# Output projection, norm, route and scatter of a mixture-of-experts layer joined into one stage, and its experts in pieces

## What is computed

```python
h = layernorm(x) * (1 + ca) + sa
x = x + ga * ((mamba(x_f) + flip(mamba(flip(x_b)))) @ w_out.T + b_out)      # two directions
h = layernorm(x) * (1 + cb) + sb
scores = softmax(h @ wg)                       # 8 experts
top1 = argmax(scores); rank = running count of tokens of the same expert
slot = top1 * 641 + rank                       # capacity 641, later tokens are dropped
y = gelu(buf[slot] @ W1[e] + b1[e]) @ W2[e] + b2[e]       # 128 -> 512 -> 128
x = x + gb * where(rank < 641, y[slot], 0) * scores[top1]
```

## Time and profile before

| | us |
|---|---|
| median of 3 runs | 1871.85 (1871.12 to 1874.78) |
| profiled execution | 1881.69, its span 1879.9 |
| busy: TensorE, VectorE, ScalarE, GpSimd | 1542, 1341, 1012, 1009 |
| mamba stage | 0 to 924 |
| projection and norm | 924 to 962 |
| route and scatter | 962 to 1021 |
| experts | 1021 to 1151 |
| attention, norm, experts of layer 1 | 1151 to 1880 |

### The profile page before, as it was taken

The page is one execution under the profiler, slowest core; times in us unless marked ns, Lnnn a source line. Parts: engine busy times, 40 slices in busy tenths (PEclk is TensorE's granted clock), DMA queues, the critical chain, the costliest instruction groups (busy, mean ns, idle before and its releaser), DMA issues. The chain is left out here.

```text
span 1879.9 us, 22117 instructions
## 1 busy us (share of the span) xinstructions
PE 1542.2 (82%) x7115; PEld 706.3 (38%) x7115; DVE 1341.4 (71%) x1497; ACT 1011.8 (54%) x1645; POOL 1008.5 (54%) x534
## 2 busy tenths in 40 slices
PE   7777887878878787886691886898899998899998
PEld 4222222222222222221271664554455555464443
DVE  6599999999999999999562112666666776157545
ACT  4867777777667777764230432444555555456221
POOL 1599999999999999999524333211011110025000
PEclk8899889898998989887875997879999999889999
DMA  4464443243444443333014222522333320102546
GB/s 155 102 158 103 113 102 92 81 108 81 112 113 102 113 102 94 84 98 90 26 35 113 48 67 61 143 54 63 86 87 87 85 72 20 51 1 50 120 100 139
DMA packets 101777, 164.94 MB, mean 88 GB/s; under 512 B 16678, under 2 KB 55374, under 8 KB 99990
## 3 DMA queue, kind: packets, MB, share of 16 engines
q1 hardware_dynamic: 93510, 159.07, 33.5%
q0 software_dynamic: 2688, 4.80, 0.8%
q10 hardware_dynamic: 5504, 0.09, 0.2%
HBM read 106.32 MB, written 26.04 MB: 70 GB/s over the span
## 5 line engine op out<-in xcount | busy, mean ns | idle before, releaser
L484 POOL TENSOR_TENSOR PR<-H,CS 128x1024 f32<-128x1024 f32 x256 | 598.4, 2359 | 50.9 <-DVE H L460 19.0
L460 DVE TENSOR_TENSOR_SCAN H<-DA,X 128x1024 f32<-128x1024 f32 x192 | 431.1, 2273 | 0.0
L349 PE MATMUL psY<-PR,fold 128*64 128x512 f32 x1024 | 295.4, 671 | 7.0 <-POOL PR L484 7.0
L448 DVE TENSOR_TENSOR X<-DU,psB 128x1024 f32<-128x1024 f32 x192 | 235.7, 1228 | 51.1 <-PE psB L328 25.6
L436 ACT ACTIVATE DA<-DT,negA 128x511 f32<-128x511 f32 x384 | 250.7, 710 | 1.1
L1478 ACT ACTIVATE a_PT<-a_psS 128x512 f32<-128x512 f32 x320 | 181.1, 601 | 110.3 <-PE a_psS L1382 106.2
L1525 DVE TENSOR_REDUCE a_MX<-a_psM 128x1 f32<-128x384 f32 (+3 forms) x352 | 203.6, 635 | 25.1 <-PE a_psM L1397 23.8
L1396 PE MATMUL a_psM<-a_kst,a_qst 72*128 72x512 bf16 (+3 forms) x512 | 140.2, 321 | 14.3 <-DVE a_MX L1525 10.5
L495 POOL TENSOR_TENSOR XS<-DU,BS 128x1024 f32<-128x1024 f32 x64 | 150.8, 2356 | 0.0
L298 PE MATMUL pp<-work,convW 128*128 (+1 forms) x256 | 140.8, 680 | 8.9 <-ACT pre L389 8.6
L460 DVE TENSOR_TENSOR_SCAN H<-X,XS 128x1024 f32<-128x1024 f32 x64 | 146.1, 2283 | 1.6 <-POOL XS L495 1.3
(11 more groups left out here) (293 smaller groups left out, 2624.8 us busy)
## 6 DMA issues: line engine op xcount, KB each, us to landing
CS<-c_rows SPq DMA_DIRECT2D x128, 256.0 KB, 3.9
DT<-W SPq DMA_DIRECT2D x64, 256.0 KB, 4.4
DU<-ab SPq DMA_DIRECT2D x64, 256.0 KB, 4.3
BS<-c_rows SPq DMA_DIRECT2D x64, 256.0 KB, 4.2
g_CB<-c_tok SPq DMA_DIRECT2D x32, 512.0 KB, 11.1
scratch_q<-a_partsq SPq DMA_DIRECT2D x24, 384.0 KB, 3.3
a_qst<-scratch_q SPq DMA_DIRECT2D x8, 1152.0 KB
a_kst<-scratch_k SPq DMA_DIRECT2D x24, 384.0 KB
```

Source lines behind the costliest of these rows:

```text
L349: last = nc.tensor.matmul(psY[h * HP:(h + 1) * HP, n % 2 * T:(n % 2 + 1) * T], fold[:, :], chunk(PR[n % 4], h), start=False, stop=n >= NS - 2)
L448: nc.vector.tensor_tensor(both(X[s % 2][:, :]), DU[p][:, at:at + 2, :], psB[:, :].unsqueeze(1).to_broadcast([P, 2, T]), ALU.mult).then_inc ...
L460: nc.vector.tensor_tensor_scan(H[s % 4][:, :], decay, x, 0.0, ALU.mult, ALU.add).then_inc(scan_done, 1)
L484: nc.gpsimd.tensor_tensor(both(PR[s % 4][:, :]), both(H[s % 4][:, :]), CS[q % 2][:, s // 2 % 2, :].unsqueeze(1).to_broadcast([P, 2, T]), A ...
```

## The change

- **One stage by batches.** `MambaOutputs` and `route_stage` go, and `outputs_stage` does projection, norm, choice, placing and scatter in one pipeline of 11 steps. Step n projects batch n, computes the variance and rows of batch n - 1, logits and transposes of batch n - 2; in odd steps from 3 on VectorE chooses for a group, in even ones from 4 on it places one, in pieces between the batch's own operations. b_out * gate is made once (`gb`) and added to xT by ScalarE ahead of time (`act_bias`); the residual is one VectorE operation from PSUM. GpSimd only scatters. wo, xc, rb, var, psPN and tps have one bank each, psL two. SP loads pack2 at the start, pack3 when the last projection is done.
- **Experts.** The slots are cut by pairs of experts (11, 10, 10, 10 tiles). Only the first piece is transposed ahead; the groups of pair i + 1 stand between the hidden tiles of pair i. One bank for transposes instead of two, three for results instead of two. The loops are written out. The first two experts' weights are issued by ScalarE at the start; SP issues the ids behind the slots.
- **Mamba's prologue.** Loads, ScalarE's and VectorE's steps stand in another order, Silu's table is loaded by a small activation of its own, and c_rows is always stored between DT's and DU's loads.

```diff
 # program
-            with ExitStack() as outputs:
-                layernorm_stage(nc, "ln1", W, xT, hT, modv(0, 4), modv(0, 3), (W2, ins["pack2"]),
-                                MambaOutputs(nc, outputs, W, XP, xT, modv(0, 2)))
-            route_stage(nc, W, W2, hT, slots, cw, W3, ins["pack3"])
+            outputs_stage(nc, W, W2, ins["pack2"], XP, xT, hT, mod[:, 0, 2, :], modv(0, 2), modv(0, 4), modv(0, 3), slots, cw, W3, ins["pack3"])
 # outputs_stage
+        def pe_project(pe, b):
+            if b >= 1:
+                pe.wait_ge(x_ready, b)
...
+        def pe_center(pe, b):
+            pe.wait_ge(x_ready, b + 1)
+            if b >= 1:
+                pe.wait_ge(copied, b)
...
+        def act_bias(act, b):
+            if b == 0:
+                act.wait_ge(step, 1)
+            nc.scalar.activation(tile(xT, b), tile(xT, b), ACT.Identity, bias=gb[:, b:b + 1]).then_inc(xb_ready, 1)
...
             def _(sp):
+                sp.dma_start(W2[:, :], pack2).then_inc(loaded, 16)
+                sp.wait_ge(loaded, 16)
+                sp.wait_ge(wo_ready, B)
+                sp.dma_start(W3[:, :], pack3).then_inc(loaded, 16)
...
             def _(pe):
+                for n in range(B + 3):
+                    if n < B:
+                        pe_project(pe, n)
+                    if 1 <= n <= B:
+                        pe_variance(pe, n - 1)
+                    if 2 <= n <= B + 1:
+                        pe_tokens(pe, n - 2)
+                    if n < B:
+                        pe_center(pe, n)
+                    if placed_at(n) is not None:
+                        pe_counts(pe, placed_at(n))
+                    if 1 <= n <= B:
+                        pe_rows(pe, n - 1)
...
             def _(act):
+                act_bias(act, 0)
+                for n in range(B + 2):
+                    if n + 1 < B:
+                        act_bias(act, n + 1)
+                    if 1 <= n <= B:
+                        act_deviation(act, n - 1)
+                    if 2 <= n <= B + 1:
+                        act_tokens(act, n - 2)
+                    if chosen_at(n) is not None:
+                        act_exp(act, chosen_at(n))
+                    if n < B:
+                        act_square(act, n)
+                    if 1 <= n <= B:
+                        act_shift(act, n - 1)
...
             def _(dve):
+                def residual(b):
+                    dve.wait_ge(wo_ready, b + 1)
+                    dve.wait_ge(xb_ready, b + 1)
+                    v.scalar_tensor_tensor(tile(xT, b), wo[:, :], gate(b), tile(xT, b), ALU.mult, ALU.add).then_inc(x_ready, 1)
...
+                for n in range(B + 3):
+                    if n < B:
+                        residual(n)
...
+                    if 1 <= n <= B:
+                        reciprocal(n - 1)
+                    if chosen_at(n) is not None:
+                        choose_exponents(chosen_at(n))
+                    if n < B:
+                        centered(n)
+                    if chosen_at(n) is not None:
+                        choose_top(chosen_at(n))
+                    if placed_at(n) is not None:
+                        place_counts(placed_at(n))
+                    if 1 <= n <= B:
+                        scale_rows(n - 1)
+                    if chosen_at(n) is not None:
+                        choose_hot(chosen_at(n))
+                    if placed_at(n) is not None:
+                        place_slots(placed_at(n))
 # experts_stage
+        psO = [ctx.enter_context(nc.psum_tensor(f"psO{i}", [P, P], F32)) for i in range(3)]
...
+                for g in range(len(groups[0])):
+                    pe_slots(pe, 0, g)
+                for i in range(E0 // 2):
+                    pe.wait_ge(sT_ready, known[i + 1])
+                    for q in range(2):
+                        pe.wait_ge(w_loaded[q], 48 * i + 48)
+                        for n in range(2):
+                            pe_hidden(pe, 2 * i + q, n)
+                            if i + 1 < E0 // 2 and 2 * q + n < len(groups[i + 1]):
+                                pe_slots(pe, i + 1, 2 * q + n)
+                    for q in range(2):
+                        pe_results(pe, 2 * i + q)
 # mamba_stage, prologue
-                load_x(1)
-                load(2, w_in, xproj)
+                load(2, w_in, xproj)
+                load_x(1)
+                load(3, xproj, WIDTH1)
                 load_x(2)
                 load_x(3)
-                load(3, xproj, WIDTH1)
...
                 act_deviation(act, 1)
+                nc.scalar.activation(small[:, 2 * T + 1:2 * T + 2], eps, ACT.Silu).then_inc(act_made, 1)
                 act_step(act, "c0", None, 0, 0)
+                act_step(act, "c1", None, 0, 0)
+                act_step(act, "silu_u", None, 0, 0)
                 act_square(act, 2)
-                act_step(act, "c1", None, 0, 0)
                 act_deviation(act, 2)
-                act_step(act, "silu_u", None, 0, 0)
...
                 dve_center(dve, 1)
+                dve_xT(dve, 1)
                 dve_mods(dve)
-                dve_xT(dve, 1)
+                dve_xT(dve, 2)
                 dve_squares(dve, 1)
-                dve_center(dve, 2)
                 dve_normal(dve, 1)
...
+                dve_xT(dve, 3)
+                dve_center(dve, 2)
```

More of the change, by code:

```diff
@@ new lines, in pe_center, with pe_variance @@
+        def pe_center(pe, b):
+            pe.wait_ge(x_ready, b + 1)
+            if b >= 1:
+                pe.wait_ge(copied, b)
+            nc.tensor.matmul(xc[:, :], w1("center"), tile(xT, b), start=True, stop=True).then_inc(xc_ready, 1)
+        def pe_variance(pe, b):
+            pe.wait_ge(sq_ready, b + 1)
+            if b >= 1:
+                pe.wait_ge(sd_ready, b)
+            for k in range(4):
+                last = nc.tensor.matmul(var[:, k:k + 1], sq[b % 2][:, k * P:(k + 1) * P], mean, start=True, stop=True)
+            last.then_inc(var_ready, 1)
@@ new lines, in act_deviation, with act_tokens, act_exp @@
+        def act_deviation(act, b):
+            act.wait_ge(var_ready, b + 1)
+            nc.scalar.activation(four(sd, b), var[:, :], ACT.Sqrt, bias=eps).then_inc(sd_ready, 1)
+        def act_tokens(act, b):
+            act.wait_ge(tps_ready, b + 1)
+            if b == 0:
+                act.wait_ge(pad_ready, 1)
+            nc.scalar.copy(htok[:, 4 * b:4 * b + 4, 0:P], tps[:, :, :]).then_inc(htok_ready, 1)
+        def act_exp(act, q):
+            act.wait_ge(lm_ready, q + 1)
+            nc.scalar.activation(ex[q % 2][:, :, :], lm[q % 2][:, :, :], ACT.Exp).then_inc(ex_ready, 1)
@@ new lines, in pe_slots, with pe_hidden @@
+        def pe_slots(pe, i, g):
+            n, tiles = known[i] + g, groups[i][g]
+            if g == 0:
+                pe.wait_ge(s_loaded[i], 16)
+            if n >= 1:
+                pe.wait_ge(sT_ready, n)
+            for k, t in enumerate(tiles):
+                last = nc.tensor.transpose(tps[:, k, :], stok[:, t, 0:P], W[:, 0:P])
+            last.then_inc(tps_ready, 1)
+        def pe_hidden(pe, e, n):
+            q, (at, wide) = e % 2, parts[n]
+            for f in range(NF):
+                k = 8 * e + 4 * n + f
+                if k >= 4:
+                    pe.wait_ge(hs_ready, k - 3)
+                nc.tensor.matmul(psH[f][:, 0:wide], W1R[q][:, f * P:(f + 1) * P],
+                                 sT[:, e * CAP + at:e * CAP + at + wide], start=True, stop=True).then_inc(H_ready, 1)
@@ new lines, in pe_results @@
+        def pe_results(pe, e):
+            q = e % 2
+            pe.wait_ge(hs_ready, 8 * e + 8)
+            for r in range(RT):
+                rows, n = min(ROWS, CAP - r * ROWS), RT * e + r
+                if n >= 3:
+                    pe.wait_ge(yt_ready, n - 2)
+                for f in range(NF):
+                    last = nc.tensor.matmul(psO[n % 3][0:rows, :], hs[q][:, f, r * ROWS:r * ROWS + rows],
+                                            W2R[q][:, f, :], start=f == 0, stop=f == NF - 1)
+                last.then_inc(O_ready, 1)
@@ L1192, in _ @@
                 for e in range(E0):
-                    rows = slots[e * CAP:e * CAP + RT * ROWS, :].rearrange("(r p) d -> p r d", p=ROWS)
-                    act.dma_start(ids[:, e * RT:e * RT + RT, :], rows[:, :, P:ROW].bitcast(U32)).then_inc(ids_loaded, 16)
-                with act.Fori(0, E0 // 2) as i:
-                    for q in range(2):
-                        act.wait_ge(O_ready, RT * (2 * i + q) + RT)
-                        for n, (at, wide) in enumerate(parts):
-                            for f in range(NF):
-                                act.wait_ge(H_ready, 16 * i + 8 * q + 4 * n + f + 9)
-                                nc.scalar.activation(hs[q][:, f, at:at + wide], psH[f][:, 0:wide], ACT.Gelu,
-                                                     bias=B1R[q][:, f:f + 1]).then_inc(hs_ready, 1)
+                    q = e % 2
@@ new lines, in _ @@
```

(8 more changed lines are left out.)

329 lines of the change are left out of this document (163 added, 166 removed).

## The result

| | before | after |
|---|---|---|
| median of 7 runs, us | 1872.04 (1868.97 to 1885.31) | 1851.16 (1846.02 to 1861.63) |
| ratio of the runs | | 0.9885, 95% interval 0.986 to 0.9911 |
| profiled execution: span, us | 1879.9 | 1847.0 |

The change saves 20.9 us (16.7 to 26.2 by the interval); 13.8 were forecast, with a range of 1844 to 1875 that holds the time. The sign, the size of the joined stage and its inner timetable were foreseen. The prologue most likely had the wrong sign and the experts were sized too small for the chip of this result, and the two errors point the same way.

A forecast was written before the change was run, and what follows sets the result against it. Three stages in a row that share no time (projection with norm, route and scatter, experts) were taken as the bound. Joined stage -10.3, experts -4, prologue +0.5 sum to -13.8: 1871.85 to 1858.0 us, range 1844 to 1875.

The forecast's parts named there:

- its two additions: Joined stage: 3 us for clock dips (0 to 7) and 3 us for late semaphores beside scatters (0 to 6).
- timetable without additions: Joined stage: when each group's scatters start, the last ends and the stage ends, 79.9 us against 96.1 before.
- the remark that TensorE is not the bound: Joined stage, two batches: TensorE's 11.1 us plus 0.6 for counts lies beside VectorE's 12.8, if the clock holds.
- Rival (a): Joined stage falls to half clock: +22.5 us until the last scatter, 1891 in all; chance 0.18.
- clock near 1.00 in the stage's windows: Joined stage: a sign that the forecast is right; a clock near 0.5 between first and last residual would show it wrong.
- the drain of 1380 ns: Joined stage, ScalarE's table changes: by the skill page some four exposed changes would add an estimated 5.5 us.
- The opening: Experts' start: first hidden matmul at 11.4 us instead of 14.7, results of the first pair 2 us earlier.
- The sum, -4: Experts: all terms of this stage together save 4 us, bounds -10 and +4.
- the transposes of the later pairs: Experts, pairs 1 and 2: transposes between hidden tiles add 1.35 us each, +2.7 us.
- the bank: Experts: a third result bank takes away 0 to 7 us of TensorE's 7.0 us of waits, 4 taken.
- the order on ScalarE: Mamba's prologue: the new order, with Silu's table early and one more Sqrt load, gives about -0.6 us.
- the store ahead of DU's loads: Mamba's prologue: SP issues c_rows' store first, so VectorE's first product waits, +1.1 us.

The follow-up runs named there:

- Chips B: Two chips of the follow-up runs, on which the kernel before took 1851.3 and 1853.5 us.
- chips A: The result's chip and that of the last four kernels (maybe the same), on which the kernel before took 1872.0 and 1872.8 us.
- kernel with two banks: The changed kernel with two result banks instead of three in the experts' stage, on a chip B: ratio to the kernel before 0.9878.
- the stage alone: The kernel before with only the joined stage of the change, prologue and experts as before, on a chip B: ratio 0.9911, -16.5 us.
- early table: The changed kernel with a small Sqrt activation behind the square in each step with an Exp, loading Sqrt's table early: ratio to the kernel before 0.9887.
- one matmul more: The changed kernel with one extra 512-column matmul ahead of each of eight projections, on a chip A: ratio to the kernel before 0.9937.
- the whole prologue: The kernel before with the whole mamba stage of the changed kernel, joined stage and experts as before, on a chip B: ratio 0.9984, -3.0 us.

## Why the prediction was right, and where it was not

**The joined stage: right, and its two additions belong to one kind of chip.** The forecast's timetable without additions was 30.8, 43.7, 55.3, 65.4, last scatter's end 75.5, stage 79.9. Chips B show 30.9, 43.0, 55.0, 65.1, an end at 74.9 and 79.3. The two additions, +3 for late semaphores and +3 for the clock, together make what chips A add: 86.9 and 86.8 against 85.9 forecast. That they fit as a sum is luck in part, since the split was wrong. On chips A the second group is placed 2.6 us later than on B, almost all of that time with the clock at full, and the third 4.5 us more, of which the pause of 3.7 us is the most; that leaves the half clock an estimated 1 us. On B, too, a fall 3.8 us later (kernel with two banks against after) placed the last group 1.2 us earlier, but brought the last scatter forward by only 0.4. So late semaphores were put down at half of what they cost, and the clock at more. (Two small slips in the sum, 96.1 - 85.9 = 10.2 and 11.1 + 1.3 + 0.5 = 12.9, change nothing.)

**Which engine sets the pace: half wrong.** Two batches were summed as 12.8 us of VectorE against 11.7 of TensorE; 12.3 are measured (42.1 - 29.8 on B), but TensorE is busy 36.57 of the first 38.20 us in the row of the stage alone, VectorE 21.05. The step that failed is the remark that TensorE is not the bound: with single banks and one fixed order both engines wait for each other in turn, as in a ring. Taking ScalarE's table load out of VectorE's path gives nothing (1.2 us of it, early table), and one more matmul is passed on by two thirds in the first group and nine tenths in the second (one matmul more). That the total came out near 12.8 all the same is luck.

**Rival (a), the half clock: no.** The granted clock is 1.00 in the first 38 us on either kind of chip; it fell to half 43 to 44 us after the start on chips A (50 with one matmul more) and 50 to 54 on B, when the projections were over. Over the second window it is 0.58 (0.64 on B), so the sign "clock near 1.00 in the stage's windows" held for the first 43 us only. The rule of the Trainium skill in "TensorE: Matmul & The Clock Gate", section "A second HAM failure mode: psum-queue depth-cycling", by which small idle times between groups of matmuls make the clock go up and down, would have given 1865 to 1885, had single banks caused such idle times; no such fall is seen while the projections run. As to the drain of 1380 ns that the Trainium skill counts in "ScalarE: Activation LUTs", section "What ACT_TABLE_LOAD costs": the load at 942.48 is followed by the deviation at 943.77, 1.29 us later, so none is seen here either.

**The experts: the size was right only where semaphores are on time.** The opening was forecast well: first hidden matmul 11.4 (11.1 measured), first gelu 12 to 14 (13.9), first results 2 earlier (2.8 on A, 2.0 on B by the means). One step in it was wrong: Gelu's table is not loaded ahead, since ScalarE's first activation stands behind its wait for the first hidden matmul (1016.21), so 1.28 us are still exposed. The sum, -4, was measured as -2.8 on chips B (-1.5 to -3 in the stage), but two of its terms were wrong and cancel, which is luck. From the first result to the last store the old code takes 75.2 to 75.6 us there and the new one 75.0 to 75.1: the transposes of the later pairs, put at +2.7, and the bank, put at -4, both come to nothing. On chips A it is 123.3 against 112.5 to 118.0, so -5 to -11 by one profile of the old code, of which some 4 are the earlier gelu. The rest was to be the third bank's, but TensorE's waits for VectorE's adds didn't go away. The forecast also read only the waits that name VectorE's add, 7.0 us, and passed over 6.9 more before the same tiles. The term that was mis-sized is that of the late semaphores: the old loop took 23 us more on A than on B (123.3 - 100.3), the new one 14 to 20. Which edit makes this difference stays open.

**The prologue: most likely the wrong sign.** Forecast +0.5; the whole prologue gives -3.0 us timed (-6.7 to +0.7), and over the profiles of all kernels the first projection stands at 918.6 us (nine, 916.5 to 923.5) with the new prologue and at 922.5 (three, 921.3 to 924.6) with the old: -3.9. Two steps failed. The first is the order on ScalarE, put at -0.6: VectorE's first product comes at 59.6 to 61.7 us with the new prologue and at 61.1 to 62.8 with the old, 1.5 us earlier by the means although the store holds it back by 1.1, so the other edits are worth some -2.6 there. (The table load ahead of the first unit's exp starts at 39.7 us in after and at 43.6 in before.) The second is the store ahead of DU's loads: its 1.1 us on VectorE are exact, but I followed only VectorE. GpSimd has as much to do in this stage (between 200 and 900 us it is busy 674.6 us, VectorE 673.3, in the kernel with the stage alone), started last, and waited for the very rows that this store sends. It starts some 4 us earlier with all of the new prologue (64.3 to 66.4 against 68.4 to 70.5), 2.1 of them by the store. How much of this reaches the end of the stage is argued from both engines being full, and not shown.

**The sum.** Against 20.9 us measured: stage 9 to 10, prologue 3 to 4, experts 5 to 11. The forecast's 13.8 lacked the prologue's part and up to half or more of what the experts give on such a chip. It lies within the range because the largest part, the stage, was right.

## What to carry to other kernels

Follow an edit of a queue to every engine that is full and to its own last input: the transfer that is moved ahead may be what the other full engine lacks. Before a wait is taken out of the path of one engine, look for what stands behind it in the ring: where another engine is busy 96% of the stretch, as TensorE is here, the wait may only change its name. (That less work on that engine would pay is likely, but no run tried it.) What paid was the overlap of the scatters, worth 29 us here. And where a kernel's gaps are pauses without cause in the program, time both versions on more than one chip; the experts' edit shortened its stage by 1.5 to 3 us on one kind and by 5 to 11 on the other.

## What was not expected of the hardware

- Chips differ in a way that repeats to 0.2 us in the joined stage. On chips A VectorE starts 1.7 to 3.3 us after the matmul that it waits for has ended, while GpSimd's indirect transfers run; on chips B it starts at once. The pauses are 1.8 to 4.5 us in the joined stage and mostly 2.5 to 4 in the experts, and the same kernel takes 20 us more (1872 against 1851). With these pauses both the joined stage (+7.6) and the experts (+14 to +23) are longer; the mamba stage is not: its first projection comes in the same range on both. What delays the signals isn't in the traces, and that the indirect transfers are the cause is read from when the pauses come; no run took them away on a chip A.
- The same mamba code ends anywhere between 916.5 and 923.5 us, though its first product varies by only 2.2 us (59.6 to 61.7).
- Half clock at a stage's start can be bought off: five matmuls of 321 columns (5.03 us), while the slots were awaited, had the next transposes at full speed. Nine of 512 columns some 10 us earlier did not: the granted clock was back at 0.50 before the slots' load.
